# The last stage of a two-layer kernel: the router as a streamed product in column tiles, and the row pairs added ahead of the turn

## What is computed

```python
logits = xf @ Wr                                   # 128 -> 8 experts
scores, experts = jax.lax.top_k(softmax(logits), 2)
scores = scores / jnp.maximum(scores.sum(-1, keepdims=True), 1e-09)
y_fb = gelu(xf @ fw1 + fb1) @ fw2 + fb2            # for tokens over the capacity
for e in range(8):
    eligible = (experts == e).any(-1) & ~fb_mask
    rank = jnp.cumsum(eligible) - 1
    keep, overflow = eligible & (rank < CAP), eligible & (rank >= CAP)
    fb_mask = fb_mask | overflow
    y = jnp.where(overflow[:, None], y_fb, y)
    idx = the kept tokens, at most CAP
    y = y.at[idx].add((gelu(xf[idx] @ W1[e] + b1[e]) @ W2[e] + b2[e]) * w_e[idx])
x = x + gb * y
```

## Time and profile before

| | |
|---|---|
| median of 3 runs | 2113.4 us (2113.12 to 2114.38) |
| the profiled execution | 2113.59 us, its span 2111.8 us |
| busy share of the span | PE 86%, VectorE 70%, ScalarE 52%, GpSimd 30% |
| mean granted clock of PE | 0.94 of full speed |
| the last stage | from 1950.8 us to the end, 161 us |

### The profile page before, as it was taken

How to read it: one execution, slowest core, us unless ns; L and a number is a source line. 1 busy time by engine, 2 the same in 40 slices (tenths; PEclk the granted TensorE clock), 3 DMA queues, 4 the chain that set the end, 5 groups by cost and what they waited for, 6 DMA issues and landing times. The chain is left out here.

```text
span 2111.8 us, 32607 instructions
## 1 busy us (share of the span) xinstructions
PE 1812.9 (86%) x12025; PEld 651.1 (31%) x12025; DVE 1473.7 (70%) x3100; ACT 1108.3 (52%) x1385; POOL 634.2 (30%) x771
## 2 busy tenths in 40 slices
PE   6445799999999999999599968888888888886989
PEld 3113233333333333333234311211211211113556
DVE  5874666666666666664334589999999999973633
ACT  4303144454444444445234238888887888884332
POOL 0031444554544454442034103302402500000152
PEclk9777699999999999999799969999999999998799
DMA  4000000000000000001021101211221211103114
GB/s 129 0 1 1 0 12 22 23 28 26 22 22 22 22 22 22 32 23 32 19 108 57 53 1 47 103 51 42 73 81 52 72 64 50 42 20 107 60 34 136
DMA packets 62331, 91.58 MB, mean 43 GB/s; under 512 B 21636, under 2 KB 38276, under 8 KB 62044
## 3 DMA queue, kind: packets, MB, share of 16 engines
q1 hardware_dynamic: 60604, 85.81, 12.0%
q0 software_dynamic: 1280, 2.62, 0.4%
q10 hardware_dynamic: 288, 1.05, 0.2%
HBM read 46.10 MB, written 38.51 MB: 40 GB/s over the span
## 5 line engine op out<-in xcount | busy, mean ns | idle before, releaser
L1575 DVE TENSOR_REDUCE h_m_half<-h_ps_max 128x1 f32<-128x512 f32 x1024 | 637.3, 683 | 35.0 <-PE h_ps_max L1284 31.4
L1460 ACT ACTIVATE h_P<-h_ps_st 128x1024 f32<-128x1024 f32 x512 | 497.7, 1023 | 86.9 <-PE h_ps_st L1300 84.2
L941 ACT ACTIVATE l_P<-l_ps_st 128x1024 f32<-128x1024 f32 (+3 forms) x384 | 306.6, 809 | 293.0 <-PE l_ps_st L821 292.0
L821 PE MATMUL l_ps_st<-l_Q,l_K 64*128 64x512 f32 (+3 forms) x1536 | 330.5, 510 | 1.2 <-DMA l_Q<-l_m_row 1.2
L1019 DVE CUSTOM_DVE_ANT_0 l_masked<-l_ps_t,l_mask 128x384 bf16<-128x384 f32 (+3 forms) x512 | 230.3, 487 | 79.4 <-PE l_ps_t L779 77.9
L1284 PE MATMUL h_ps_max<-h_K,h_Q 48*128 48x512 bf16 x1024 | 204.1, 395 | 81.1 <-DVE h_m_half L1575 78.2
L1310 PE MATMUL h_ps_o<-h_P,h_V 128*9 128x512 f32 x2048 | 268.6, 596 | 0.7 <-ACT h_P L1460 0.5
L1022 DVE TENSOR_REDUCE l_m_half<-l_ps_t 128x1 f32<-128x512 f32 x256 | 164.9, 686 | 97.0 <-PE l_ps_t L779 96.9
L990 POOL TENSOR_SCALAR_AFFINE_SELECT l_P<-l_P 128x256 f32<-128x256 f32 x256 | 102.9, 407 | 381.7 <-ACT l_P L941 381.2
L1300 PE MATMUL h_ps_st<-h_Q,h_K 51*128 51x512 bf16 x1024 | 168.0, 380 | 15.6 <-ACT h_P L1460 11.4
L1284 PEld LDWEIGHTS h_ps_max<-h_K,h_Q 48*128 48x128 bf16 x1024 | 49.4, 93 | 405.7 <-DVE h_m_half L1575 388.6
(11 more groups left out here) (387 smaller groups left out, 2211.3 us busy)
## 6 DMA issues: line engine op xcount, KB each, us to landing
sums<-l_o SPq DMA_DIRECT2D x15, 512.0 KB, 2.7
sums<-h_o SPq DMA_DIRECT2D x15, 512.0 KB, 2.6
h_K<-k_parts SPq DMA_DIRECT2D x32, 192.0 KB
h_Q<-q_parts SPq DMA_DIRECT2D x32, 192.0 KB
y_rows<-zero SPq DMA_DIRECT2D x8, 512.0 KB, 4.9
h_b<-h_a SPq DMA_DIRECT2D x32, 128.0 KB, 2.0
c_W<-in_W SPq DMA_DIRECT2D x16, 256.0 KB, 6.0
c_back<-y_rows SPq DMA_DIRECT2D x16, 256.0 KB, 5.1
```

What stands on the lines that cost most here:

```text
L821: last = pe.matmul(ps_st[x % 2][:, a, 0:w], K[n // NG % 2][rows, kt * 128:(kt + 1) * 128], Q[n % NQ][rows, c, p, q0 - c * CH:q0 - c * CH + ...
L941: act.activation(P[e % PR][:, :, 0:w], ps_st[slot["s", n, i, p] % 2][:, :, 0:w], ACT.Exp, scale=0.125).then_inc(consumed, 1)
L1460: act.activation(P[e % PR][:, :, :], ps_st[x % 2][:, :, :], ACT.Exp, scale=1.0 / 12.0).then_inc(consumed, 1)
L1575: dve.tensor_reduce(m_half[:, half, 2 * p + a, qt:qt + 1], ps_max[:, t % NB, :], AX.X, ALU.max, negate=True)\
```

## The change

It touches the last stage alone, in three parts.

- **Router.** `Wr` is padded with zeros to 32 columns. In two halves c, PE streams the tokens through four groups of 32 columns of the array, into `ps_h[0]`; the tokens of a half are taken from `hT` in runs of four (16 bytes) with a step of 32. ScalarE copies each half to `across` (the memory of `hidden[1]`), PE turns it in four transposes into `ps_t[c]`, and VectorE copies each half to the logits. The wait of PE for the copy stands now behind `up(0, 1)`, ahead of `row_group(0)`.
- **Row pairs.** `pair_rows(eng, c)` adds the two rows of every token of a chunk on GpSimd (even chunks, behind the scatters in its queue) or VectorE (odd chunks). PE has one transpose for 128 tokens where it had two products.
- **Loads.** A partition takes four neighbouring rows of `y_rows`, 2 KB in one piece, where it took four pieces of 512 bytes. The transposes write every fourth column of `ps_t` in exchange.

```diff
+        def pair_rows(eng, c):
+            eng.wait_ge(landed[c], 32)
+            one, two = [YB[:, k, 4 * c:4 * c + 4, :].rearrange("p t d -> p (t d)") for k in range(2)]
+            eng.tensor_tensor(one, one, two, ALU.add).then_inc(paired[c % 2], 1)
...
-                    sp.dma_start(YB[:, k, 4 * c:4 * c + 4, :], S.y_rows[lo:lo + CH, :].rearrange("(t p) d -> p t d", p=128)).then_inc(landed[c], 16)
+                    sp.dma_start(YB[:, k, 4 * c:4 * c + 4, :], S.y_rows[lo:lo + CH, :].rearrange("(p t) d -> p t d", p=128)).then_inc(landed[c], 16)
...
             def sum_rows(c):
                 if c >= 2:
                     pe.wait_ge(joined, c - 1)
-                pe.wait_ge(landed[c], 32)
+                pe.wait_ge(paired[c % 2], c // 2 + 1)
                 for i in range(4):
-                    for k in range(2):
-                        last = pe.matmul(ps_t[c % 2][:, i * 128:(i + 1) * 128], YB[:, k, 4 * c + i, :], S.ident[:, :], start=(k == 0), stop=(k == 1))
+                    last = pe.transpose(ps_t[c % 2][:, i:CH:4], YB[:, 0, 4 * c + i, :], S.ident[:, :])
...
-            for i in range(NT):
-                last = pe.matmul(ps_y[0][:, i * X:(i + 1) * X], S.hT[:, i:N:NT], Wr[:, :], start=True, stop=True)
-            last.then_inc(routed, 1)
+            by_row = S.hT[:, :].rearrange("d (p t) -> d p t", t=NT)
+            for c in range(2):
+                for j in range(4):
+                    last = pe.matmul(ps_h[0][32 * j:32 * j + 32, c, :], Wr[:, :], by_row[:, :, 8 * j + 4 * c:8 * j + 4 * c + 4], start=True, stop=True)
+                last.then_inc(across_made, 1)
+            for c in range(2):
+                pe.wait_ge(across_kept, c + 1)
+                for k in range(4):
+                    last = pe.transpose(ps_t[c][:, k * 128:(k + 1) * 128], across[:, c, k:CH:4], S.ident[:, :])
+                last.then_inc(routed, 1)
...
             up(0, 0)
             up(0, 1)
+            pe.wait_ge(chain, 2)
             row_group(0)
...
+            for c in range(2):
+                act.wait_ge(across_made, c + 1)
+                act.activation(across[:, c, :], ps_h[0][:, c, :], ACT.Identity).then_inc(across_kept, 1)
...
+            for c in range(0, NC, 2):
+                pair_rows(pool, c)
...
             for c in range(NEARLY, NC):
                 add_fb(c)
+                if c == NEARLY:
+                    pair_rows(dve, 1)
             for c in range(NC):
+                if c % 2 == 0 and c + 3 < NC:
+                    pair_rows(dve, c + 3)
                 dve.wait_ge(summed, c + 1)
```

More of the change, by code:

```diff
@@ L2159, in capacity_weights @@
     W.W1, W.W2 = sb("W1", [D, X + 1, 4, 128]), sb("W2", [128, X + 1, 4, D])
-    W.Wr, W.b2, W.table = sb("Wr", [D, X]), sb("b2", [128, X, D]), sb("table", [128, 2 * X + 3 * 128 + X * CAP // 128 + 1])
+    W.Wr, W.b2, W.table = sb("Wr", [D, 32]), sb("b2", [128, X, D]), sb("table", [128, 2 * X + 3 * 128 + X * CAP // 128 + 1])
     W.loaded, W.fb_loaded, W.experts_loaded = [semaphore(nc, ctx, "c_" + x) for x in ("loaded", "fb_loaded", "experts_loaded")]
@@ L2224, in capacity_experts @@
         hidden = [sb(f"hidden{i}", [128, F, CH]) for i in range(2)]
+        across = hidden[1][:, 0:2, :]
         y_fb = [sb(f"y_fb{i}", [D, CH]) for i in range(NEARLY)]
@@ L2230, in capacity_experts @@
         set_, rows_turned, rows_kept, rows_stored = [sem(x) for x in ("set", "rows_turned", "rows_kept", "rows_stored")]
+        across_made, across_kept = sem("across_made"), sem("across_kept")
         based, matched, weighted = [sem(x) for x in ("based", "matched", "weighted")]
@@ L2236, in capacity_experts @@
         up_done, gelu, down_done, fb_kept, fb_masked, fb_added = [sem(x) for x in ("up", "gelu", "down", "fb_kept", "fb_masked", "fb_added")]
+        paired = [sem("paired_by_pool"), sem("paired_by_dve")]
         x_turned, x_kept, y_made, summed, joined, stored = [sem(x) for x in ("x_turned", "x_kept", "y_made", "summed", "joined", "stored")]
         block = ctx.enter_context(nc.Block())
+        def pair_rows(eng, c):
+            eng.wait_ge(landed[c], 32)
+            one, two = [YB[:, k, 4 * c:4 * c + 4, :].rearrange("p t d -> p (t d)") for k in range(2)]
+            eng.tensor_tensor(one, one, two, ALU.add).then_inc(paired[c % 2], 1)
         @block.sync
@@ L2356, in _ @@
             up(1, 1)
-            pe.wait_ge(chain, 1)
             fb_down(0, 0)
@@ L2474, in _ @@
             dve.wait_ge(bias_made, 4)
-            dve.wait_ge(routed, 1)
-            link(dve.tensor_copy(logits[:, :, :], ps_y[0][:, 0:NT * X].rearrange("p (t x) -> p t x", x=X)))
+            for c in range(2):
+                dve.wait_ge(routed, c + 1)
+                link(dve.tensor_copy(logits[:, :, :].rearrange("p (j c k) x -> p c j k x", j=4, c=2)[:, c],
+                                     ps_t[c][:, :].rearrange("p (k j w) -> p j k w", k=4, j=4)[:, :, :, 0:X]))
             for k in range(2):
@@ L2680, in layout @@
         "Wu_k": paired(i["L1_attn_Wu_k_w"]), "Wu_v": i["L1_attn_Wu_v_w"], "bvG": i["L1_attn_Wu_v_b"].reshape(D, 1),
-        "WoG1": beside(i["L1_attn_Wo_w"], beside(i["L1_attn_Wo_w"][96:].reshape(HG, 8 * D), np.zeros((HG, 24 * D))).reshape(128, D)), "Wr": i["L1_ffn_Wr"], "b2": i["L1_ffn_b2"].reshape(1, X * D), "W1": i["L1_ffn_W1"], "W2": i["L1_ffn_W2"],
+        "WoG1": beside(i["L1_attn_Wo_w"], beside(i["L1_attn_Wo_w"][96:].reshape(HG, 8 * D), np.zeros((HG, 24 * D))).reshape(128, D)), "Wr": beside(i["L1_ffn_Wr"], np.zeros((D, 32 - X))), "b2": i["L1_ffn_b2"].reshape(1, X * D), "W1": i["L1_ffn_W1"], "W2": i["L1_ffn_W2"],
         "fw1": i["L1_ffn_fw1"], "fw2": i["L1_ffn_fw2"],
```

## The result

The changed kernel takes **2103.3 us** (median of 5 runs, 2102.28 to 2104.14) against 2113.12 us (5 runs, 2111.73 to 2114.38): ratio 0.9954, 95% interval 0.9942 to 0.9967. The forecast was 2104.0. Measured again later, the same two kernels gave 0.9958 (0.9942 to 0.9974). The profiled execution took 2102.28 us, its span is 2100.5, 11.3 less than before.

The account below looks back on a forecast made before the run. PE was taken to bound the last stage: 14.01 us of router products, the experts, 14.66 us adding and turning pairs. Terms -7.5 and -1.9 sum to -9.4 from 2113.4, giving 2104.0 us, range 2098.5 to 2109.

Parts of the forecast that it names:

- Part 1: Router: streamed products start VectorE's first reduction 8.7 us earlier, less 1.2 for clock; term -7.5 us (-8.7 to -3.4).
- the half clock in the limits: Limits after the router: products take 0.58 us instead of 0.38, up to 0.2 for each of six, 1.2 us.
- the stretch behind them: Work behind the limits: starts at half clock as now; costs 1.5 us more if the rise comes 3 us later.
- The term's bound of -3.4: Router: the smallest gain allowed for the term, with the clock costing up to 5.3 us.
- the doubled stream: Router: reading tokens in 16-byte runs with a step might take up to twice 3.64 us; 3.64 was assumed.
- Everything up to 2085 follows VectorE's last limit and moves with it.: Between limits and join: the router's whole gain, -7.5 us, carries through because the chain behind the limits is untouched.
- Rival C: Experts: late signals move with new timing; gone gives 2097.4 us (chance 0.06), longer gives 2110.6 us (chance 0.05).
- one of the prediction's own signs of being wrong: Experts: their 8 us of standing still gone or grown would show the prediction wrong.
- Part 2: Join's loads: 2 KB pieces run at 370 GB/s instead of 292 and chunk 7 lands at 2101.7.
- Rival B: Join's loads get no faster, chunk 7 lands at 2104.7, Part 3 becomes +1.1; 2107.0 us, chance 0.12.
- Part 3: Join: pairs on GpSimd and VectorE, one PE transpose per 128 tokens, last join ends at 2105.7; term -1.9 us.
- Contention: Join: VectorE and GpSimd pairs may delay each other; counted 0, with 1.3 us kept for the range.

Follow-up runs that it names:

- warm_to_the_end: Changed kernel plus unread PE products ahead of the first limit and behind all limits but the last; 2090.7 us, ratio 0.9944 to the kernel before.
- after_again: The changed kernel itself, unaltered, measured again beside the kernel before on another occasion; 2102.4 us, ratio 0.9958.
- pair_late: Changed kernel with each VectorE pair just ahead of its own join, not two chunks ahead; 2106.2 us, ratio 0.9968 to the kernel before.
- group 2: One chip: changed kernel again, pairs moved later, unread products at the limits, gathers spaced; ratios 0.9927 to 0.9968, kernel before 2112.8 us.
- groups 1 and 3: Eight other follow-up kernels, four per chip, each beside the kernel before, which took 2104.1 and 2101.7 us there.
- group 1: One chip: router alone, join alone, 512-byte loads, PE adding pairs with 2 KB loads; ratios 0.9957 to 0.9986, kernel before 2104.1 us.
- pairs_512: Changed kernel with loads in 512-byte pieces and transposes into blocks of 128 columns; 2097.7 us, ratio 0.9976 to the kernel before.
- join_only: Kernel before with only the new row pairs, transposes and 2 KB loads, router as before; 2101.0 us, ratio 0.9986 to the kernel before.

## Why the prediction was right, point by point

- **Part 1, -7.5 us.** The reduction came 8.8 us earlier (8.7 forecast), the half clock in the limits took 1.1 (1.2), the stretch behind them, up to the end of the inversion, 0.5 (counted 0, up to 1.5). Without late signals the router gives 7.6 us, by one trace of either router. The term's bound of -3.4 held the clock alone; the doubled stream that the prediction allowed for would have taken 3.6 more. As forecast, the clock was at 1.00 ahead of the first limit and lost in the limits. By warm_to_the_end half clock costs 4.4 us from the first limit on; 1.6 of them are new with the change, the rest the kernel before paid too, whose clock fell after six limits and stood at 0.50 behind them.
- **"Everything up to 2085 follows VectorE's last limit and moves with it."** This step failed wherever signals were late: the stage is shorter by 4.6, 4.8 and 2.1 us in the first trace, in after_again and in pair_late, not by 7.5. Rival C had the place and, in the last two, the kind: the standing still grew, one of the prediction's own signs of being wrong. In the first trace it kept its length, and half clock behind it took 2.6 us more than before; C had half clock at 2.2 us, but only as part of a pause that goes or grows. All three differences lean on the one trace of before, so that their size is uncertain.
- **Part 2.** 370 GB/s was taken, 395 measured in the middle of the join; chunk 7 at 14.1 us, not 14.4. Rival B, that the loads get no faster, falls with the rate.
- **Part 3, -1.9 us.** Measured -2.0, with its inner steps: pairs of 0.69 and 1.27, four joins in 3.6 us behind the last landing. PE's turns ran mostly at half clock, 1.97 us for two chunks, a little over the bound of 0.92 each. Contention was counted at 0, and rightly for the sum: the chunks land 1.4 us apart and in the first trace no pair on VectorE begins before the one on GpSimd has ended. Where one did, both grew, with nothing lost at the end (join 17.84); timeline of after_again:

```profile
2083.38 1.78 POOL L2246 TENSOR_TENSOR c_back<-c_back 128x512 f32<-128x512 f32 x1 [2.19 <-DMA c_back<-y_rows]
2084.71 1.00 DVE L2246 TENSOR_TENSOR c_back<-c_back 128x512 f32<-128x512 f32 x1 [0.67 <-DMA c_back<-y_rows]
```

- **The total.** -6.9 of the -11.3 us in the spans are from the stage; 4.4 came from unchanged code ahead of it, where the starts scatter by 6 us. The medians, -9.8 and -10.4, lie at the forecast's -9.4, but where signals are late the traces hold only 6.9 of it. 6.9 us would be a ratio of 0.9967, at the upper end of the first interval and inside the second, so noise can hold the 3 us between. They stay open: the trace of before is one execution, and how long the late signals were in its others isn't known. That the profiled execution comes out at the forecast is luck: the 4.4 us of scatter made up for what the stage fell short. Where no signals are late, the terms and the medians agree within the intervals.

## What to carry to other kernels

Read the granted clock on both sides of every wait that you shorten or move: PE that arrives early and waits can pay at half clock for several microseconds what the earlier arrival won. Unread products in all the gaps gave 4.4 us here in the traces and 2.6 in the medians; with one gap of 0.8 us left open, next to nothing. Two halves of a pipeline change (faster loads, work taken off the engine that they would expose) can each be worth nothing, as here, and together be worth 1.5 to 2 us. When two traces are compared, subtract stage by stage: here 4.4 us of the 11.3 between the spans were scatter ahead of it. And where a wait scatters by several microseconds from one execution to the next, a single trace of it before and after does not price a change.

## What the runs showed of the hardware that was not expected

- Signals of PE that the other engines see 2 to 12 us after the records of its products (12 in pair_late, a turn recorded until 2019.0 and released at 2031.34): in all six traces of the first measurement and of group 2, in none of the eight of groups 1 and 3, so that it seems to come with the chip. The last of a spell is released 1.4 to 3.5 us behind the end of an unbroken row of GpSimd's indirect DMA issues, and moved with it once. The gathers landed in 2.7 us (median) in the changed kernel's first trace, in 2.5 in group 1. What holds the signals back is not shown.
- A stationary operand of 32 columns and a moving one in runs of 16 bytes with a step of 128: 3.64 us for 16 records of 512 columns, as in layer 0's router, which reads no such runs. Transposes into every fourth column: 1.97 us for eight at half clock, as into a block.
- 290 GB/s for loads in 512-byte pieces (pairs_512), 395 in 2 KB pieces (the changed kernel, and join_only on the chip of pairs_512). The Trainium skill (DMA: Bandwidth & Descriptors, Specifications) gives 512 bytes as the least size for line rate; by these stretches 2 KB is a third faster still.
